# Dense products two chunks at a time in 64-row tiles of TensorE, in a transformer layer on one core

## The chip, the core and the metric
The kernel runs on one core of one Trainium2 chip. TensorE (PE) multiplies, VectorE (DVE), ScalarE (ACT) and GpSimd (POOL) work on its results, and SyncE (SP) issues most transfers. The time is device microseconds of one execution of the program; the kernel before took 677.64 us, the median of three runs (675.79 to 679.14).

## What is computed
For each of 8 rows of 512 tokens x 256 channels, all in float32:

```python
xn = _layernorm(x, axis=-1)
qkv = xn @ qkv_w + qkv_b                       # 16 heads of 16 channels
attn = softmax(einsum('bnhd,bmhd->bhnm', q, k) * scale)
out = einsum('bhnm,bmhd->bnhd', attn, v) @ proj_w + proj_b
gate = xn @ wg.T; up = xn @ wu.T               # 768 hidden, integer weights / 127
ffn = (silu(gate) * up) @ wd.T
x = x + out + ffn
```

## The kernel before
All engines run the same plan. A row has 16 steps: step s handles key tile s % 4 of the head group s // 4, which has four heads in two pairs. A step has two halves, one for each pair of heads. In a half PE computes transposed scores (`scores_t`, L733, into `st_bank`), which ACT turns into `probs` (`exp`, L454), and, six steps ahead (`LEAD`), plain scores (`scores`, L750, into `s_bank`), of which DVE takes the maxima (`maxima`, L575). Each of these is a pair of matmuls in the two 64-row tiles of the array, one for each head, in two banks. `s_bank` and `st_bank` exist once, so the next scores wait for DVE, and the next transposed scores for ACT. Between the halves stands `P @ V` (`probs_v`, L764), in 32-column tiles. The four maxima groups of a row (`max`) are transposed, split and sent by DMA into the rows of `q_stack` that the transposed scores read.

The rest of the layer is cut into chunks: `xn` (transposes of the normalised row), `q`, `k`, `v`, `gate`, `up`, `down`, `proj`, `max`, `o` and `ot` (transposes of the attention's output). A chunk fills one of three banks (`dense`), in turn, by the order of the list `STEADY` (for the first row, in which only chunks and the first scores run, `FIRST`). An entry (step, slot, kind, index, offset) puts the chunk in slot 0 (before the first half), 1 (before the second) or 2 (after it) of a step, for the row at that offset. The same table orders PE, ACT, DVE and POOL: in each slot ACT and DVE first do their part of the half (`exp`; `maxima`), then take the chunks (`take`). A gate chunk is taken by a tanh on ACT (L484) and a product on DVE (L625, `gated`); an up chunk by a product on DVE (L633, `hid`), whose high part ACT copies (L503) and whose low part POOL makes (L413); q and k by ACT (L470) and DVE (L591). DVE's release of a chunk counts in `dense_free`, and a chunk that wants a bank waits for the release of the chunk three before it (L784).

A product is split into exact high and low parts in fp32r, by the list `SPLIT`. As the integer weights are exact in one part, rows 0 to 7 use two terms for gate, up and down, in place of three. `product` (L769) issues a chunk's matmuls one behind the other over all 128 rows of the array. In the first row ACT also squares the low parts of the three integer weights (`square_lows`, L497), by which that is decided, behind `wdown` 2.

## Time and profile before
| | |
|---|---|
| median of 3 runs | 677.64 us |
| profiled execution, its own time | 674.83 us |
| its span | 673.0 us |
| mean granted TensorE clock | 0.987 |
| PE / DVE / ACT / POOL busy | 93 / 74 / 57 / 20% |
| first row's part (before the first exp) | 60.9 us |
| row 0, rows 1 to 6 each, row 7 | 74.3, 77.3 to 78.2, 60.7 us |
| after the last full step | 12 us |

The span runs from the first to the last instruction. PE's busy time is made of modelled ends of pipelined matmuls, which overlap, so the start-to-start distance of matmuls tells more than their length: a row of the timeline with x2 holds two that follow each other, or, for `st_bank` and `s_bank`, two in the two row tiles at once. `PEld` are weight loads.

### The profile page before, as it was taken

The page shows a single profiled execution, that of the slowest core. Times are in us where ns is not written, and L with a number is a line of the kernel's source. Part 1 is how long each engine was busy: PE and PEld are TensorE (multiplying, and loading weights), DVE is VectorE, ACT ScalarE, POOL GpSimd, SP SyncE. Part 2 cuts the span into 40 slices and gives each one's busy share as a digit, 9 for nine tenths or more (in the row PEclk, how much of TensorE's full clock was granted, in tenths as well). Part 3 has the DMA queues.
Part 4 walks back from the last instruction along what each step waited for, and adds up shares of the span by engine and source line. Part 5 has one row for each costly group of instructions (what it writes and reads, how often), then busy time and mean ns, then how long its engine had stood idle before and what let it go on. Part 6 is the DMA issues. An engine that isn't in the chain of part 4 may idle for free.

```text
span 673.0 us, 11305 instructions
## 1 busy us (share of the span) xinstructions
PE 627.3 (93%) x3792; PEld 349.0 (52%) x3792; DVE 498.6 (74%) x676; ACT 383.8 (57%) x499; POOL 133.8 (20%) x134
## 2 busy tenths in 40 slices
PE   6848999999899999999999999999999999999996
PEld 5625545545555555545454555555465455555443
DVE  4758777877778877778778778777778777787732
ACT  2533664756556655656557555566647565566563
POOL 3151113210142004211133002411132101021100
PEclk9868999999999999999999999999999999999999
DMA  8750154112812145111831037211640118120201
GB/s 276 211 106 1 34 164 123 25 38 95 220 49 48 30 150 134 47 48 46 244 72 46 3 127 186 48 48 32 183 127 21 48 63 220 49 48 2 65 2 34
DMA packets 38076, 59.12 MB, mean 88 GB/s; under 512 B 5792, under 2 KB 21152, under 8 KB 38048
## 3 DMA queue, kind: packets, MB, share of 16 engines
q1 hardware_dynamic: 36896, 58.22, 31.4%
q10 hardware_dynamic: 1152, 0.52, 0.3%
q8 instruction: 18, 0.29, 0.2%
q14 instruction: 10, 0.08, 0.0%
HBM read 37.23 MB, written 20.97 MB: 86 GB/s over the span
## 4 chain that ended last, share of the span: by engine, by line
PE 75%; DVE 9%; ACT 5%; issue 5%; DMA 3%; SPq 1%; ACTq 0%; DVEq 0%
PE dense L774 33%; PE o_bank L764 15%; PE st_bank L733 13%; PE s_bank L750 9%; DVE neg_max L575 4%; DMA q_stack<-max_tl 2%; ACT probs L454 2%; PE dense L810 1%; DMA p_bias<-in_L_attn_proj_b 1%; ACT qk_parts L470 1%; SPq L305 1%; PE dense L788 1%; DVE hid L633 1%; PE dense L814 1%; PE dense L805 1%
## 5 line engine op out<-in xcount | busy, mean ns | idle before, releaser
L454 ACT ACTIVATE probs<-st_bank 128x1024 f32<-128x1024 f32 x250 | 256.0, 1024 | 199.6 <-PE st_bank L733 194.5
L575 DVE TENSOR_REDUCE neg_max<-s_bank 128x2 f32<-128x1024 f32 x250 | 305.5, 1222 | 74.7 <-PE s_bank L750 73.8
L764 PE MATMUL o_bank<-probs,v_ones 128*32 128x512 f32 x1024 | 136.4, 605 | 4.3 <-ACT probs L454 2.4
L733 PE MATMUL st_bank<-q_stack,k_stack 50*128 50x512 f32 x500 | 125.0, 496 | 8.8 <-ACT probs L454 4.3
L750 PE MATMUL s_bank<-k_stack,q_stack 48*128 48x512 f32 x500 | 110.0, 436 | 13.8 <-DVE neg_max L575 13.6
L413 POOL TENSOR_TENSOR hid_tl<-hid,hid_th 128x512 fp32r<-128x512 f32 x48 | 61.7, 1285 | 307.6 <-ACT hid_th L503 307.6
L733 PEld LDWEIGHTS st_bank<-q_stack,k_stack 50*128 50x128 f32 x500 | 46.8, 183 | 125.4 <-ACT probs L454 82.3
L750 PEld LDWEIGHTS s_bank<-k_stack,q_stack 48*128 48x128 f32 x500 | 47.5, 186 | 36.6 <-DVE neg_max L575 34.0
L625 DVE SCALAR_TENSOR_TENSOR gated<-gated,dense 128x512 f32<-128x512 f32 x48 | 32.9, 686 | 21.6 <-ACT gated L484 20.9
L764 PEld LDWEIGHTS o_bank<-probs,v_ones 128*32 128x32 f32 x1024 | 20.3, 108 | 50.7 <-issue 46.9
L427 POOL TENSOR_TENSOR resid<-resid,p_bias 128x256 f32<-128x256 f32 x32 | 22.4, 733 | 121.0 <-DMA resid<-in_L_attn_x 121.0
L591 DVE SCALAR_TENSOR_TENSOR qk_parts<-dense,qk_bias,qk_parts 128x512 fp32r<-128x512 f32 x32 | 23.9, 751 | 20.8 <-ACT qk_parts L470 20.8
L484 ACT ACTIVATE gated<-dense 128x512 f32<-128x512 f32 x48 | 28.6, 595 | 13.8 <-PE dense L774 13.8
L503 ACT ACTIVATE hid_th<-hid 128x512 fp32r<-128x512 f32 x48 | 30.0, 626 | 9.1 <-DVE hid L633 9.1
L774 PE MATMUL dense<-xn_th,w_gh 128*128 128x512 f32 x96 | 34.3, 439 | 0.3 <-DVE w_dl L649 0.3
L405 POOL TENSOR_SCALAR xn<-xn,moments,rstd 128x256 f32<-128x256 f32 x28 | 33.8, 1221 | 1.2 <-POOL rstd L399 1.2
L633 DVE SCALAR_TENSOR_TENSOR hid<-dense,gated 128x512 f32<-128x512 f32 x48 | 32.7, 682 | 0.4
L470 ACT ACTIVATE qk_parts<-dense,qk_bias 128x512 fp32r<-128x512 f32 x32 | 21.8, 685 | 19.5 <-PE dense L774 14.1
L774 PE MATMUL dense<-w_dh,hid_th 128*128 128x256 f32 x192 | 31.4, 299 | 0.0
L774 PE MATMUL dense<-xn_th,w_uh 128*128 128x512 f32 x96 | 31.1, 405 | 0.0
L774 PE MATMUL dense<-xn_tl,w_gh 128*128 128x512 f32 x96 | 30.5, 399 | 0.0
L774 PE MATMUL dense<-xn_tl,w_uh 128*128 128x512 f32 x96 | 29.9, 392 | 0.0
(101 smaller groups left out, 708.5 us busy)
## 6 DMA issues: line engine op xcount, KB each, us to landing
q_spread<-qk_parts SPq DMA_DIRECT2D x16, 512.0 KB, 3.0
k_spread<-qk_parts SPq DMA_DIRECT2D x16, 512.0 KB, 3.5
q_stack<-q_spread SPq DMA_DIRECT2D x64, 128.0 KB, 3.1
k_stack<-k_spread SPq DMA_DIRECT2D x64, 128.0 KB, 3.2
q_stack<-q_spread SPq DMA_DIRECT2D x64, 64.0 KB, 3.2
k_stack<-k_spread SPq DMA_DIRECT2D x64, 64.0 KB, 3.2
resid<-in_L_attn_x SPq DMA_DIRECT2D x8, 512.0 KB, 4.9
xn<-in_L_attn_x SPq DMA_DIRECT2D x7, 512.0 KB, 3.5
```

What stands on the lines that cost most here:

```text
L405: nc.gpsimd.tensor_scalar(xn[:, t, :], xn[:, t, :], moments[:, t, 0:1], rstd[:, t:t + 1], ALU.subtract, ALU.mult).then_inc(xn_done, 1)
L413: nc.gpsimd.tensor_tensor(hid_t[1][:, m, :], hid[:, m % 2, :], hid_t[0][:, m, :].bitcast(F32), ALU.subtract).then_inc(hid_low, 1)
L454: nc.scalar.activation(probs[:, s % 2, 2 * half:2 * half + 2, :], transposed_bank(row, s, half)[:, :, :], ACT.Exp, scale=SCALE).then_inc(e ...
L484: nc.scalar.activation(gated[:, i % 2, :], bank[:, :], ACT.Tanh, scale=0.5 * QUANT).then_inc(act_done, 1)
L503: nc.scalar.activation(hid_t[0][:, m, :], hid[:, m % 2, :], ACT.Copy).then_inc(hid_high, 1)
L575: nc.vector.tensor_reduce(neg_max[:, g % 2, :, NT * pair + qt], score_bank(row, half)[:, :, :], AX_X, ALU.max, negate=True).then_inc(max_d ...
L625: nc.vector.scalar_tensor_tensor(gated[:, i % 2, :], gated[:, i % 2, :], 1.0, bank[:, :], ALU.add, ALU.mult).then_inc(dense_free, 1)
L633: nc.vector.scalar_tensor_tensor(hid[:, i % 2, :], bank[:, :], 0.5 * QUANT ** 3, gated[:, i % 2, :], ALU.mult, ALU.mult).then_inc(dense_fr ...
L733: done = nc.tensor.matmul(transposed_bank(row, s, half)[:, r, :], k_stack[rows, pair, P * kt:P * (kt + 1)], q_stack[rows, pair, :], start= ...
L750: done = nc.tensor.matmul(score_bank(row, half)[:, r, :], q_stack[rows, pair, P * qt:P * (qt + 1)], k_stack[rows, pair, :], start=True, st ...
L764: done = nc.tensor.matmul(o_bank[32 * j:32 * (j + 1), :], v_ones[:, kt, HG * g + j, :], probs[:, (s - 1) % 2, j, :], start=kt == 0, stop=k ...
L774: done = nc.tensor.matmul(bank, stationary(a, k), moving(b, k), start=n == 0 and k == 0, stop=n == len(parts) - 1 and k == tiles - 1)
```

## The change
Dense products are no longer made a chunk at a time over the whole array. Two chunks that go together (gate and up of one index, q and k of one index, v 0 and 1, proj 0 and 1, down 0 and 1, 2 and 3) are made at once in the two 64-row tiles: in the first half the upper rows of the contraction go to the bank of the first chunk and the lower rows to that of the second; in the second half the tiles swap banks. So a bank is never written by both tiles at once, and the second half waits for the end of the first (`half_done`). There are as many matmuls again, of 64 rows. Both chunks are done together, with the last matmul (`dense_done` + 2). A table `WORK` of its own now says where PE works: for v, proj and down the two halves stand in different steps, for gate/up and q/k in one block. v's first half stands at the end of the row before. `STEADY` still orders the other engines and the banks. The transposes of `xn`, `o` and `ot` move to slot 1, behind `P @ V`, and `gate` 4 moves from the row before into step 1. In the first row wdown's transposes stand ahead of q 1 and k 1, gate 1 comes at step 10, gate 4 goes, and the squarings stand behind gate 1.

```diff
-    (11, 0, "gate", 0, 1), (11, 2, "down", 3, 0),
-    (12, 0, "up", 0, 1), (12, 2, "gate", 1, 1),
...
+    (9, 1, "o", 1, 0), (10, 1, "max", 3, 0),
+    (10, 2, "down", 2, 0), (11, 0, "down", 3, 0),
+    (11, 2, "gate", 0, 1), (12, 0, "up", 0, 1),
...
+WORK = [
...
+    (7, 2, "down", 0, 0, 0),
+    (8, 2, "down", 0, 1, 0),
+    (9, 1, "o", 1, None, 0), (9, 2, "down", 2, 0, 0),
+    (10, 1, "max", 3, None, 0), (10, 2, "down", 2, 1, 0),
+    (11, 2, "gate", 0, None, 0),
...
+TOGETHER = {
+    ("v", 0): ("v", 1), ("q", 0): ("k", 0), ("q", 1): ("k", 1), ("proj", 0): ("proj", 1),
+    ("down", 0): ("down", 1), ("down", 2): ("down", 3), **{("gate", i): ("up", i) for i in range(KH)},
+}
...
-SQUARES_AFTER = ("wdown", 2)
+SQUARES_AFTER = ("gate", 1)
...
-            def product(bank, stationary, moving, tiles, parts=SPLIT, moving_low=None):
-                for n, (a, b) in enumerate(parts):
-                    if b == 1 and moving_low is not None:
-                        pe.wait_ge(dense_free, moving_low)
-                    for k in range(tiles):
-                        done = nc.tensor.matmul(bank, stationary(a, k), moving(b, k), start=n == 0 and k == 0,
-                                                stop=n == len(parts) - 1 and k == tiles - 1)
+            def product(terms, half, low=None):
+                for (stationary, moving, bank), first, last, moves_low in terms:
+                    if low is not None and moves_low and half == 0:
+                        pe.wait_ge(dense_free, low)
+                        low = None
+                    done = []
+                    for r in range(2):
+                        c = (r + half) % 2
+                        rows = slice(HALF * r, HALF * (r + 1))
+                        done.append(nc.tensor.matmul(bank[c], stationary[c][rows], moving[c][rows],
+                                                     start=first and half == 0, stop=last and half == 1,
+                                                     tile_position=(HALF * r, 0)))
                 return done
-            def chunk_products(row, chunk, exact):
-                _, _, kind, i, offset = chunk
+            def terms_of(banks, stationary, moving, tiles, parts=SPLIT, column=0, columns=1):
+                return [(([stationary(c, a, k) for c in range(2)], [moving(c, b, k) for c in range(2)], banks),
+                         column == n == k == 0,
+                         column == columns - 1 and n == len(parts) - 1 and k == tiles - 1, b == 1)
+                        for n, (a, b) in enumerate(parts) for k in range(tiles)]
+            def bank_free(row, chunk):
+                if count(Row(row.like, row.like), ALL, chunk) > DENSE_BANKS:
+                    pe.wait_ge(dense_free, count(row, ALL, chunk) - DENSE_BANKS)
+            def two_chunks(row, kind, i, half, exact):
+                (one,), (two,) = named(row, kind, i), named(row, *TOGETHER[kind, i])
+                banks = [bank_of(row, c) for c in (one, two)]
+                if half != 1:
+                    bank_free(row, two)
+                whole = [b[:, :] for b in banks]
+                low = None
+                if kind == "q":
+                    if i == 0:
+                        pe.wait_ge(act_done, count(row, ON_ACT, kind="xn", index=1))
+                        low = count(row, ALL, kind="xn", index=1)
+                    if i == 0 and row.like == -1:
+                        pe.wait_ge(w_low, 2)
+                    terms = terms_of(whole, lambda c, a, k: w_qkv[a][:, k, C * c + P * i:C * c + P * (i + 1)],
+                                     lambda c, b, k: xn_t[b][:, k, :], KC)
+                elif kind == "v":
+                    terms = []
+                    for u in range(2):
+                        terms += terms_of([b[:, C * u:C * (u + 1)] for b in banks],
+                                          lambda c, a, k: xn_t[a][:, k, P * (2 * c + u):P * (2 * c + u + 1)],
+                                          lambda c, b, k: w_qkv[b][:, k, 2 * C:3 * C], KC, column=u, columns=2)
+                elif kind == "gate":
+                    if row.like == -1 and i == 0:
+                        pe.wait_ge(dense_free, count(row, ALL, kind="wup", index=2))
+                    terms = terms_of(whole, lambda c, a, k: (w_g, w_u)[c][a][:, k, P * i:P * (i + 1)],
+                                     lambda c, b, k: xn_t[b][:, k, :], KC, STATIONARY_EXACT if exact else SPLIT)
+                elif kind == "down":
+                    if i == 0 and half == 0:
+                        pe.wait_ge(hid_high, KH * (row.at + 1))
+                        pe.wait_ge(hid_low, KH * (row.at + 1))
+                    terms = terms_of([b[:, 0:C] for b in banks],
+                                     lambda c, a, k: hid_t[a][:, k, P * (i + c):P * (i + c + 1)],
+                                     lambda c, b, k: w_d[b][:, k, :], KH, MOVING_EXACT if exact else SPLIT)
+                else:
+                    if half == 0:
+                        pe.wait_ge(dense_free, count(row, ALL, kind="ot", index=1))
+                    terms = []
+                    for u in range(2):
+                        terms += terms_of([b[:, C * u:C * (u + 1)] for b in banks],
+                                          lambda c, a, k: ot_parts[:, k, a, P * (2 * c + u):P * (2 * c + u + 1)],
+                                          lambda c, b, k: w_p[b][:, k, :], KC, column=u, columns=2)
+                if half != 1:
+                    for done in product(terms, 0, low):
+                        done.then_inc(half_done, 1)
+                if half != 0:
+                    pe.wait_ge(half_done, 2 * count_together(row, kind, i))
+                    product(terms, 1)[1].then_inc(dense_done, 2)
+            def transposes(row, kind, i):
+                (chunk,) = named(row, kind, i)
+                offset = chunk[4]
                 bank = bank_of(row, chunk)
-                n = count(row, ALL, chunk)
...
-                for chunk in chunks_at(row, s, slot):
-                    chunk_products(row, chunk, exact)
+                for step_at, slot_at, kind, i, half, ahead in (FIRST_WORK if row.like == -1 else WORK):
+                    table = of_row(row, ahead)
+                    if (step_at, slot_at) != (s, slot) or table.like > ROWS or not named(table, kind, i):
+                        continue
+                    if (kind, i) in TOGETHER:
+                        two_chunks(table, kind, i, half, exact)
+                    else:
+                        transposes(table, kind, i)
```

How PE's instructions move. First, row 0, the blocks of gate 1 with up 1 (step 12), before. The names are the tiles: `w_gh`, `w_uh` are the weights, `xn_th`, `xn_tl` the high and low part of the transposed row.

```order
L750 MATMUL s_bank<-k_stack,q_stack 128x512 x2
L774 MATMUL dense2<-xn_th,w_gh 128x512 x2
L774 MATMUL dense2<-xn_tl,w_gh 128x512 x2
L774 MATMUL dense0<-xn_th,w_uh 128x512 x2
L774 MATMUL dense0<-xn_tl,w_uh 128x512 x2
L733 MATMUL st_bank<-q_stack,k_stack 128x512 x2
```

The same place on PE in the changed kernel, from the last pair of the first half on:

```order
L826 MATMUL dense2<-xn_tl,w_gh 128x512
L826 MATMUL dense0<-xn_tl,w_uh 128x512
L826 MATMUL dense0<-xn_th,w_uh 128x512
L826 MATMUL dense2<-xn_th,w_gh 128x512
L826 MATMUL dense0<-xn_th,w_uh 128x512
L826 MATMUL dense2<-xn_th,w_gh 128x512
L826 MATMUL dense0<-xn_tl,w_uh 128x512
L826 MATMUL dense2<-xn_tl,w_gh 128x512
L826 MATMUL dense0<-xn_tl,w_uh 128x512
L826 MATMUL dense2<-xn_tl,w_gh 128x512
L778 MATMUL st_bank<-q_stack,k_stack 128x512 x2
```

Gate's bank (`dense2`) was complete four matmuls ahead of the end; now it is written until the last matmul, like up's. Second, PE in step 13 of row 0, where `o` 2 is transposed, before:

```order
L764 MATMUL o_bank<-probs,v_ones 32x512 x4
L733 MATMUL st_bank<-q_stack,k_stack 128x512 x2
L750 MATMUL s_bank<-k_stack,q_stack 128x512 x2
L810 MATMUL dense1<-ident,o_raw 128x128 x4
L774 MATMUL dense2<-xn_th,w_gh 128x512 x2
```

and in the changed kernel:

```order
L809 MATMUL o_bank<-probs,v_ones 32x512 x4
L908 MATMUL dense1<-ident,o_raw 128x128 x4
L778 MATMUL st_bank<-q_stack,k_stack 128x512 x2
L795 MATMUL s_bank<-k_stack,q_stack 128x512 x2
L826 MATMUL dense2<-xn_th,w_gh 128x512
```

The transposes, which use the whole array, moved from the dense block to the place between `P @ V` and the 64-row pairs.

## Rows read from the trace of the kernel before
**Rows 1.** The page, part 1: busy us (share of the span) and instructions
```profile
PE 627.3 (93%) x3792; PEld 349.0 (52%) x3792; DVE 498.6 (74%) x676; ACT 383.8 (57%) x499; POOL 133.8 (20%) x134
```

**Rows 2.** Stretches: length, busy us (x) of PE, PEld, DVE, ACT, POOL, clock, DMA
```profile
290.06:305.25 15.19, 13.91 (x91) 7.58 (x91) 11.57 (x17) 8.63 (x12) 2.25 (x2) 1.00 0.15 39
305.25:325.43 20.18, 20.16 (x124) 11.53 (x123) 15.54 (x18) 12.29 (x17) 1.41 (x2) 1.00 0.26 94
325.43:344.25 18.82, 18.00 (x117) 9.95 (x116) 15.23 (x26) 9.95 (x12) 5.27 (x8) 1.00 0.72 180
344.25:367.40 23.15, 23.15 (x136) 12.12 (x135) 18.42 (x22) 15.45 (x21) 7.70 (x7) 1.00 0.17 43
...
60.92:135.20 74.28, 72.09 (x422) 38.84 (x420) 57.25 (x77) 45.14 (x58) 16.33 (x17) 0.98 0.29 80
...
600.40:661.10 60.70, 55.76 (x365) 27.98 (x363) 35.33 (x47) 37.34 (x45) 5.90 (x7) 1.00 0.11 27
```

**Rows 3.** Timeline, steps 1 and 2: start, us, engine, line, operation
```profile
298.08 0.40 PE L774 MATMUL dense<-w_qkvl,xn_th 128*128 128x256 f32 x2
...
298.32 0.40 PE L774 MATMUL dense<-w_qkvh,xn_th 128*128 128x256 f32 x2
...
300.06 0.50 PE L733 MATMUL st_bank<-q_stack,k_stack 50*128 50x512 f32 x2
300.17 0.19 PEld L750 LDWEIGHTS s_bank<-k_stack,q_stack 48*128 48x128 f32 x2
300.40 0.40 PE L750 MATMUL s_bank<-k_stack,q_stack 48*128 48x512 f32 x2
...
300.73 1.07 PE L764 MATMUL o_bank<-probs,v_ones 128*32 128x512 f32 x8
...
301.73 0.28 PE L805 MATMUL dense<-ident,neg_max 128*16 128x128 f32 x1
...
301.93 0.50 PE L733 MATMUL st_bank<-q_stack,k_stack 50*128 50x512 f32 x2
```

**Rows 4.** Timeline, steps 12 and 13 of a full row
```profile
275.80 0.60 ACT L484 ACTIVATE gated<-dense 128x512 f32<-128x512 f32 x1
275.99 0.61 PE L774 MATMUL dense<-xn_tl,w_uh 128*128 128x512 f32 x2
...
276.43 0.69 DVE L625 SCALAR_TENSOR_TENSOR gated<-gated,dense 128x512 f32<-128x512 f32 x1 [0.60 <-ACT gated L484]
...
276.54 0.50 PE L733 MATMUL st_bank<-q_stack,k_stack 50*128 50x512 f32 x2
...
277.32 1.23 DVE L575 TENSOR_REDUCE neg_max<-s_bank 128x2 f32<-128x1024 f32 x1 [0.20 <-PE s_bank L750]
...
278.46 0.68 DVE L633 SCALAR_TENSOR_TENSOR hid<-dense,gated 128x512 f32<-128x512 f32 x1
...
278.60 0.51 PE L750 MATMUL s_bank<-k_stack,q_stack 48*128 48x512 f32 x2
```

**Rows 5.** Timeline, step 0 of a full row
```profile
290.93 0.68 DVE L625 SCALAR_TENSOR_TENSOR gated<-gated,dense 128x512 f32<-128x512 f32 x1
...
291.52 1.22 DVE L575 TENSOR_REDUCE neg_max<-s_bank 128x2 f32<-128x1024 f32 x1
...
292.80 0.50 PE L750 MATMUL s_bank<-k_stack,q_stack 48*128 48x512 f32 x2 [0.55 <-DVE neg_max L575]
```

**Rows 6.** The page, part 5: DVE's half of q and k
```profile
L591 DVE SCALAR_TENSOR_TENSOR qk_parts<-dense,qk_bias,qk_parts 128x512 fp32r<-128x512 f32 x32 | 23.9, 751 | 20.8 <-ACT qk_parts L470 20.8
```

**Rows 7.** Timeline, the end of the program
```profile
669.77 0.69 DVE L645 TENSOR_TENSOR resid<-dense,resid 128x512 f32<-128x512 f32 x1 [0.74 <-PE dense L774]
```

**Rows 8.** Timeline, first row
```profile
38.40 0.69 DVE L625 SCALAR_TENSOR_TENSOR gated<-gated,dense 128x512 f32<-128x512 f32 x1 [5.58 <-ACT gated L484]
...
41.99 0.80 PE L750 MATMUL s_bank<-k_stack,q_stack 48*128 48x512 f32 x2 [7.57 <-DVE neg_max L575]
...
60.38 0.51 PE L733 MATMUL st_bank<-q_stack,k_stack 50*128 50x512 f32 x2 [0.96 <-DVE neg_max L575]
```

More of the change, by code:

```diff
@@ L138, in count, with count_together @@
     return total + sum(PER_ROW[kind] for kind in kinds) * (row.at - like)
+def count_together(row, kind, index):
+    mine = [c[2:4] for c in chunks_of(row.like) if c[2:4] in TOGETHER]
+    total = sum(c[2:4] in TOGETHER for r in range(-1, row.like) for c in chunks_of(r))
+    return total + mine.index((kind, index)) + 1 + len(TOGETHER) * (row.at - row.like)
 OFFSET = {c[2:4]: c[4] for c in STEADY}
@@ L268, in chunks_at, with named @@
             return [c for c in chunks_of(row.like) if c[:2] == (step, slot)]
+        def named(row, kind, i):
+            return [c for c in chunks_of(row.like) if c[2:4] == (kind, i)]
         def pair_ahead(row, step, half):
@@ L512, in hidden_highs, with maxima_taken @@
                                 hidden_high(r, chunk)
+            def maxima_taken(row, s, slot):
+                if slot == 0:
+                    s, slot = s - 1, SLOTS
+                return [c for c in chunks_at(row, s, slot - MAX_DELAY) if c[2] == "max"]
             def load_max(row, chunk):
@@ L539, in step @@
                                 square_lows()
-                        for chunk in chunks_at(row, s, slot - MAX_DELAY):
-                            if chunk[2] == "max":
-                                load_max(row, chunk)
+                        for chunk in maxima_taken(row, s, slot):
+                            load_max(row, chunk)
                         if slot == 1 and s % NT == 0 and 0 < STEPS * row.like + s <= STEPS * ROWS:
@@ L780, in chunk_products @@
+            def transposes(row, kind, i):
+                (chunk,) = named(row, kind, i)
+                offset = chunk[4]
                 bank = bank_of(row, chunk)
-                n = count(row, ALL, chunk)
-                if count(Row(row.like, row.like), ALL, chunk) > DENSE_BANKS:
-                    pe.wait_ge(dense_free, n - DENSE_BANKS)
+                bank_free(row, chunk)
                 if kind == "xn":
@@ L788, in chunk_products @@
                         done = nc.tensor.transpose(bank[:, P * t:P * (t + 1)], xn[:, t, P * i:P * (i + 1)], ident[:, :])
-                elif kind in ("q", "k"):
-                    if kind == "q" and i == 0:
-                        pe.wait_ge(act_done, count(row, ON_ACT, kind="xn", index=1))
-                    if i == 0 and row.like == -1:
-                        pe.wait_ge(w_low, 1 if kind == "q" else 2)
-                    base = (0 if kind == "q" else C) + P * i
-                    low = count(row, ALL, kind="xn", index=1) if kind == "q" and i == 0 else None
-                    done = product(bank[:, :], lambda a, k: w_qkv[a][:, k, base:base + P],
-                                   lambda b, k: xn_t[b][:, k, :], KC, moving_low=low)
-                elif kind == "v":
-                    for u in range(2):
-                        t = 2 * i + u
-                        done = product(bank[:, C * u:C * (u + 1)], lambda a, k: xn_t[a][:, k, P * t:P * (t + 1)],
-                                       lambda b, k: w_qkv[b][:, k, 2 * C:3 * C], KC)
                 elif kind == "max":
@@ L815, in chunk_products @@
                                                    ident[:, :])
-                elif kind in ("gate", "up"):
-                    w = w_g if kind == "gate" else w_u
-                    if kind == "gate" and count(Row(row.like, row.like), ("gate",), chunk) == 1:
-                        pe.wait_ge(dense_free, count(Row(-1, -1), ALL, kind="wup", index=2))
-                    done = product(bank[:, :], lambda a, k: w[a][:, k, P * i:P * (i + 1)],
-                                   lambda b, k: xn_t[b][:, k, :], KC, STATIONARY_EXACT if exact else SPLIT)
-                elif kind == "down":
-                    if i == 0:
-                        pe.wait_ge(hid_high, KH * (row.at + 1))
-                        pe.wait_ge(hid_low, KH * (row.at + 1))
-                    done = product(bank[:, 0:C], lambda a, k: hid_t[a][:, k, P * i:P * (i + 1)],
-                                   lambda b, k: w_d[b][:, k, :], KH, MOVING_EXACT if exact else SPLIT)
-                elif kind == "proj":
-                    if i == 0:
-                        pe.wait_ge(dense_free, count(row, ALL, kind="ot", index=1))
-                    for u in range(2):
-                        t = 2 * i + u
-                        done = product(bank[:, C * u:C * (u + 1)], lambda a, k: ot_parts[:, k, a, P * t:P * (t + 1)],
-                                       lambda b, k: w_p[b][:, k, :], KC)
                 elif kind == "wdown":
```

43 lines of the change are left out of this document (27 added, 16 removed), and 17 rows, old and new, of tables (FIRST, STEADY).

## The prediction
> **What bounds the kernel now.** I read the busy times first: PE is busy 93% of the span [rows 1]. Then a table by stage of one of the six full rows (77.3 us each): steps 0 to 2 take 15.19 us, 3 to 6 20.18, 7 to 10 18.82, 11 to 15 23.15; row 0 takes 74.3 us and row 7 60.7 [rows 2]. PE is nearly gap-free in the last three stages, DVE is second at 60.8 of 77.3 us. Then the timeline, start to start, for what PE's time is made of. Full-array products of 512 columns follow each other every 0.23 us, of 256 columns every 0.12 [rows 3, 4]. The pairs of 64-row tiles behave otherwise when they follow another shape: `st_bank` starts 0.32 after the last dense matmul, its weights are then loaded in the open (the load for `s_bank` begins 0.11 later), and `s_bank` starts 0.34 after it, though only 0.23 after its own load began; `P @ V` starts 0.33 after that; from its start to what follows is 1.00 [rows 3, 4]. So a change of tile shape costs about 0.2 us (0.1 to drain, 0.1 of open weight load), and each step ends with two of them, 64-row to full and back.
>
> **The change, part by part.**
> Dense products in 64-row tiles. Both changes at the end of each step go: 2 x 0.2 = 0.39 us, 16 times a row: -6.3 us. The pairs are taken at 0.23 (512 columns) and 0.12 (256), as full-array products are. Bounds: 0.23 below, as nothing in the rows streams 512 columns faster, and 0.34 above, if the load is never hidden [rows 3]; I take 0.23, since the load of `s_bank` began 0.11 after `st_bank` in the same row tiles and cost nothing more. On this the Trainium skill (TensorE: Matmul & The Clock Gate, "The mechanism") is stricter: a weight load overlaps matmuls in flight only when the row group differs. The rows speak against that rule here; by it every pair would cost 0.11 more, which is a rival below.
>
> Halves. A half waits until the other half of the same two banks is done. Where other work stands between (v, proj, down) this is free. For six gate/up and two q/k blocks it stands inside the block: the last matmul takes 0.40 from start to end, 0.05 for the hand-over, 0.11 for an open load, in place of 0.23: +0.32, 8 times: +2.6 us. Bounds: 0 to 0.4 each.
>
> Small transposes beside `P @ V`. There they sit between a 32-column and a 64-row shape: six more visits at 0.2 us: +1.2 us; the four of `max` were there already [rows 3]. PE's own work so falls by 2.5 us a row: by these distances it is 72.8 now (the other 4.5 are waits) and 70.3 then.
>
> What comes late instead. A gate and its up product now finish together. Before, gate was done 0.93 us ahead of the end of the block, and its tanh (0.60) ran beside up [rows 4]. Now, counted from the end D of the block: tanh 0.05 to 0.65, DVE `gated` from 0.68, DVE maximum from 1.28 to 2.51 (a DVE instruction behind another starts 0.1 before the end of the first), and the second `s_bank` of the step, which waits for that maximum, at 2.56. PE alone would be there at -0.165 + 0.23 + 0.33 + 1.00 + 0.34 = 1.73. So PE waits 0.83 us in each of the six steps after a gate block. Step 0 of before shows it, where the gate product is already the last of a block: `gated` runs first on DVE, the maximum starts at 291.52 behind it, and the next `s_bank` waits 0.55 for it [rows 5]. A gate block is then 0.34 + 3 x 0.23 + 0.45 + 0.11 + 3 x 0.23 + 0.40 = 2.68 from `s_bank` to D, so a step takes 5.24, where it took 4.5 to 4.9.
>
> Banks. Two chunks need two of three banks at once, so a block waits for the release of the chunk three before its second. In steps 13, 14 and 15 that is `hid` of the last block, at 2.41 + 0.68 = 3.09 on DVE [rows 4]: the block starts at 3.14 with an open load, D at 5.59. In step 2 it is `max` (5.78), in step 3 the low half of the first `xn` (5.46), in step 6 k of the last block (DVE 0.75 each [rows 6]: 6.74), in step 9 `o`, since down's half now stands ahead of it (4.81). Transfers: those of the `max` rows are issued by ACT behind q 1 as now, and are needed at step 8; I count nothing for them, as the block before and step 7 cover them, and if they land late the cost is a wait at the first `st_bank` of step 8.
>
> Sum. Worked through in this way the steps are: 0 to 2: 3.80, 5.35, 5.78 = 14.93 (before 15.19); 3 to 6: 5.46, 3.73, 5.81, 6.74 = 21.74 (20.18); 7 to 10: 4.65, 3.70, 4.81, 3.77 = 16.93 (18.82); 11 to 15: 4.47, 5.24, 5.59, 5.59, 4.85 = 25.74 (23.15). Together 79.3 against 77.3: **+2.0 us a row**. Steps with no release in the way gain 0.4 to 1, those behind gate and q/k lose as much. Six rows: +12. Row 0 has no `o`, `ot`, `proj` of a row before, so it had less to gain and has the same gate blocks: +3. Row 7 has no gate 0 to 3 and no q/k: -2. The end: both proj chunks finish together, so the first 0.69 us addition no longer runs beside the second product [rows 7], and one open half wait: +1.
>
> First row. Before, three squarings on ACT stand ahead of gate 1's tanh, DVE waits 5.58 us for it, and PE then 7.57 for the first maximum [rows 8]. They move behind gate 1, and that wait goes. But wdown now stands ahead of q 1 and k 1, gate 0 ends some 6 us later by my count, and each later gate ends with its up, behind which DVE waits for tanh, and v's first half is added. I come out at 60.4 us for the first score of row 0, where it is now [rows 8]: 0, between -6 (the wait goes and nothing replaces it) and +3.
>
> Total +14 us on the profiled execution, whose own time is 674.8 us (span 673.0, 1.8 us around it). The median of the runs is 677.6, 2.8 above it. 674.8 + 14 is 689; half the offset added: **690 us**.
>
> **Rivals.**
> A, forecast: the freed time is spent in waits for releases and in half waits. 678 to 708, as a row comes out at +0.5 to +4.
> B, PE's saved changes are kept for the most part: the tanh chain is overlapped better than I think (ACT is busy only 57% of the time [rows 1]), and q/k and proj steps come out at PE's time. PE's own sum with the present waits is 2.5 us a row less, 17 in seven rows: 657 with nothing from the first row, 651 with its 6; without any wait it would be 626. For it: 16 changes a row are certain to go, and PE is the busy engine. Against it: step 0 of before [rows 5], where this order of events already stalls.
> C, both sides cancel: within 0.5% (3.4 us, about what a measurement of this kernel can tell from no change). 675 to 681.
> D, weight loads of 64-row tiles aren't hidden in a long stream: 0.11 more for each pair. A row has 72 pairs of 512 and 96 of 256 columns, some 120 of them on the path: +13 us a row, some 780. Against it: rows 3. For it: no stretch of this trace has more than two such pairs in a row, nor four instructions in 0.12 us for long.
> E, the 0.2 us isn't a matter of shape but of any hand-over between these products: nothing goes, +6.3 us a row more than in A, some 735. Against it: full-array products of different tiles follow at 0.12 and 0.23 without a gap.
>
> **Chances.** A 0.53, D and E together 0.08: slower 0.61. C 0.12 is no change, B 0.27 faster. The range: 0.1 of the chance lies under 652 (the better part of B), 0.1 above 714 (D, E and a row at +5). A's own range is 678 to 708.
>
> **What would show it.** Right: rows of 78 to 81 us; the two shape changes gone (dense to `st_bank` 0.23, `st_bank` to `s_bank` 0.23 at the start of a step); steps 12 to 15 of 5.2 to 5.6 us with PE idle before the second `s_bank`, put down to DVE `neg_max`, some 0.8 us each; a pause of 0.2 to 0.3 us inside gate/up and q/k; DVE waits for `gated` about 0.7 us in each gate step; step 6 the longest. PE busy under 90%. Wrong: rows under 76 us, or no PE wait on `neg_max` in steps 12 to 15; then the chain from tanh to the maximum is not on the path. Pair spacing of 0.34 inside a block would make it D, 0.34 after a dense block E. A first row that ends before 57 us would show that the late gate 0 costs nothing.

## The result, and the profile after

The changed kernel takes 713.99 us (median of four runs, 710.60 to 717.77) against 677.26 for the kernel before: a ratio of 1.054, 95% interval 1.048 to 1.060. It is slower, as forecast, but by 36.7 us where the forecast had 12.7 (690 less 677.3). Its profiled execution has a span of 711.3 us, 38.3 more than before. One run of e12 below, 770.6 us, was in a slower state of the chip and is left out there.

The busy times and the chain of waits of the kernel after, against [rows 1]:

```profile
span 711.3 us, 14030 instructions
## 1 busy us (share of the span) xinstructions
PE 625.4 (88%) x5150; PEld 352.8 (50%) x5150; DVE 492.9 (69%) x676; ACT 385.0 (54%) x499; POOL 133.7 (19%) x134
...
## 4 chain that ended last, share of the span: by engine, by line
PE 57%; DVE 15%; issue 12%; ACT 9%; DMA 4%; ACTq 1%; DVEq 1%; POOL 0%; SPq 0%; POOLq 0%
PE dense L826 35%; PE o_bank L809 8%; DVE neg_max L620 6%; PE st_bank L778 6%; PE s_bank L795 5%; ACT gated L524 4%; DMA q_stack<-max_tl 4%; DVE hid L678 3%; ACT probs L494 2%; ACT qk_parts L510 1%; PE dense L908 1%; DVE qk_parts L636 1%; DVE xn_tl L631 1%; ACTq L566 1%; DVE stats L602 1%
```

PE does the same work in the same busy time and stands idle for 12% of the span instead of 7%; its share of the chain falls from 75 to 57%. The table by stage of one full row of the kernel after, then row 0 and row 7, answers to [rows 2], columns as there (a stage begins with the first `st_bank` product of its step; row 0 and row 7 from their first exponential):

```profile
226.59:241.89 15.30, 14.23 (x117) 7.76 (x115) 11.85 (x17) 8.66 (x12) 2.43 (x2) 1.00 0.15 41
241.89:263.97 22.08, 20.59 (x175) 11.88 (x173) 15.39 (x19) 11.95 (x16) 1.30 (x1) 1.00 0.28 96
263.97:282.62 18.65, 15.98 (x169) 9.68 (x165) 14.23 (x23) 10.22 (x12) 4.05 (x7) 1.00 0.66 170
282.62:308.46 25.84, 23.82 (x183) 12.26 (x180) 18.48 (x23) 15.55 (x21) 8.80 (x8) 1.00 0.15 39
65.49:146.60 81.11, 73.08 (x570) 39.42 (x568) 57.22 (x77) 45.41 (x59) 16.27 (x17) 0.96 0.27 74
636.60:697.78 61.18, 52.27 (x457) 26.89 (x455) 35.14 (x47) 37.70 (x45) 6.12 (x7) 1.00 0.10 27
```

This row takes 81.87 us, in stages of 15.30, 22.08, 18.65 and 25.84, where the forecast had 14.93, 21.74, 16.93 and 25.74. In the sum of the span the 38.3 us lie so: up to the first exponential 65.5 us instead of 60.9 (+4.6), row 0 81.1 instead of 74.3 (+6.8), rows 1 to 6 490.0 instead of 465.2 (+24.8), row 7 61.2 instead of 60.7 (+0.5), the end 13.5 instead of 12.0 (+1.5).

A step behind a gate block in the timeline of the kernel after (start, duration, engine and line, what it writes and reads; in brackets the idle time before it and what ended it):

```profile
286.88 0.39 PE L826 MATMUL dense<-xn_tl,w_gh 64*128 64x512 f32 x1
...
287.11 0.39 PE L778 MATMUL st_bank<-q_stack,k_stack 50*128 50x512 f32 x2
...
287.32 0.60 ACT L524 ACTIVATE gated<-dense 128x512 f32<-128x512 f32 x1 [1.59 <-PE dense L826]
...
287.94 0.69 DVE L670 SCALAR_TENSOR_TENSOR gated<-gated,dense 128x512 f32<-128x512 f32 x1 [1.61 <-ACT gated L524]
288.55 1.22 DVE L620 TENSOR_REDUCE neg_max<-s_bank 128x2 f32<-128x1024 f32 x1
...
289.82 0.50 PE L795 MATMUL s_bank<-k_stack,q_stack 48*128 48x512 f32 x2 [0.44 <-DVE neg_max L620]
...
290.17 0.39 PE L826 MATMUL dense<-xn_th,w_gh 64*128 64x512 f32 x1
...
290.40 0.39 PE L826 MATMUL dense<-xn_th,w_gh 64*128 64x512 f32 x1
290.40 0.18 PEld L826 LDWEIGHTS dense<-xn_tl,w_gh 64*128 64x128 f32 x1
...
290.63 0.39 PE L826 MATMUL dense<-xn_tl,w_gh 64*128 64x512 f32 x1
...
290.86 0.39 PE L826 MATMUL dense<-xn_tl,w_gh 64*128 64x512 f32 x1
...
291.34 0.18 PEld L826 LDWEIGHTS dense<-xn_th,w_uh 64*128 64x128 f32 x1 [0.52 <-PE dense L826]
...
292.37 0.39 PE L778 MATMUL st_bank<-q_stack,k_stack 50*128 50x512 f32 x2
```

This is the forecast's chain, event by event. The block ends at 287.27 (286.88 + 0.39); tanh at +0.05, `gated` at +0.67, the maximum at +1.28, the second `s_bank` at +2.55 (forecast 2.56). The pairs follow at 0.23; between the halves PE's queue stands until 291.34, 0.48 after the last pair; from dense to `st_bank` it is 0.23 where [rows 3] had 0.32. The step takes 5.26 us (forecast 5.24). The waits of the kernel after, in total, times and longest:

```profile
DVE gated L670 <- ACT gated L524: 78.1, 47, 3.5
...
DVE qk_parts L636 <- ACT qk_parts L510: 46.4, 23, 4.8
...
PEld dense L826 <- PE dense L826: 34.3, 65, 0.8
...
PEld st_bank L778 <- DMA q_stack<-max_tl: 6.6, 5, 2.1
```

DVE waits 78.1 us for tanh; in the kernel before it was 20.9; for the q and k takes 46.4, before 20.8. The last line is the wait for the max rows, which the forecast priced at nothing. It is not new. The same view of the kernel before has:

```profile
PEld st_bank L733 <- DMA q_stack<-max_tl: 5.2, 4, 2.0
```

What such a wait costs in either kernel is the matter of e1 and e7. In the row above it looks so:

```profile
264.18 0.69 ACT L510 ACTIVATE qk_parts<-dense,qk_bias 128x512 fp32r<-128x512 f32 x1 [3.54 <-PE dense L826]
264.18 0.51 ACTq L566 DMA_DIRECT2D q_stack<-max_th  x1
...
264.72 0.52 ACTq L566 DMA_DIRECT2D q_stack<-max_tl  x1
...
265.42 1.02 ACT L494 ACTIVATE probs<-st_bank 128x1024 f32<-128x1024 f32 x1 [0.56 <-issue]
...
270.05 0.19 PEld L778 LDWEIGHTS st_bank<-q_stack,k_stack 50*128 50x128 f32 x2 [1.42 <-DMA q_stack<-max_tl]
```

ACT issues the two transfers of the max rows behind its take of q 1. That product now ends with k 1, so they go out at 264.18 and 264.72, among the stack transfers; the exponential of step 7 stands 0.56 us behind their issue, and `st_bank` of step 8 waits 1.42 for the second.

### The profile page after: what moved, and what is told of

It is laid out like the page before. It is cut to its first block, busy times and chain, and to the rows that moved or that the text cites. A ratio compares the mean times of both kernels' runs of the same rounds, so it can differ in the third digit from the quotient of the medians.

```text
span 711.3 us, 14030 instructions
## 1 busy us (share of the span) xinstructions
PE 625.4 (88%) x5150; PEld 352.8 (50%) x5150; DVE 492.9 (69%) x676; ACT 385.0 (54%) x499; POOL 133.7 (19%) x134
## 4 chain that ended last, share of the span: by engine, by line
PE 57%; DVE 15%; issue 12%; ACT 9%; DMA 4%; ACTq 1%; DVEq 1%; POOL 0%; SPq 0%; POOLq 0%
PE dense L826 35%; PE o_bank L809 8%; DVE neg_max L620 6%; PE st_bank L778 6%; PE s_bank L795 5%; ACT gated L524 4%; DMA q_stack<-max_tl 4%; DVE hid L678 3%; ACT probs L494 2%; ACT qk_parts L510 1%; PE dense L908 1%; DVE qk_parts L636 1%; DVE xn_tl L631 1%; ACTq L566 1%; DVE stats L602 1%
## 5 line engine op out<-in xcount | busy, mean ns | idle before, releaser
L809 PE MATMUL o_bank<-probs,v_ones 128*32 128x512 f32 x1024 | 138.0, 611 | 8.0 <-ACT probs L494 4.7
L778 PE MATMUL st_bank<-q_stack,k_stack 50*128 50x512 f32 x500 | 113.8, 451 | 21.4 <-ACT probs L494 14.3
L670 DVE SCALAR_TENSOR_TENSOR gated<-gated,dense 128x512 f32<-128x512 f32 x48 | 33.0, 687 | 78.1 <-ACT gated L524 78.1
L826 PE MATMUL dense<-xn_th,w_gh 64*128 64x512 f32 x192 | 68.6, 437 | 6.0 <-DVE max_tl L653 2.0
L826 PE MATMUL dense<-xn_th,w_uh 64*128 64x512 f32 x192 | 68.6, 437 | 4.3
L826 PE MATMUL dense<-xn_tl,w_gh 64*128 64x512 f32 x192 | 60.5, 395 | 0.0
L826 PE MATMUL dense<-xn_tl,w_uh 64*128 64x512 f32 x192 | 60.5, 395 | 0.0
L636 DVE SCALAR_TENSOR_TENSOR qk_parts<-dense,qk_bias,qk_parts 128x512 fp32r<-128x512 f32 x32 | 23.8, 749 | 46.4 <-ACT qk_parts L510 46.4
L826 PEld LDWEIGHTS dense<-xn_th,w_uh 64*128 64x128 f32 x192 | 30.8, 189 | 25.7 <-PE dense L826 25.6
L826 PEld LDWEIGHTS dense<-xn_th,w_gh 64*128 64x128 f32 x192 | 30.9, 189 | 15.2 <-DVE hid L678 6.2
L826 PEld LDWEIGHTS dense<-xn_tl,w_gh 64*128 64x128 f32 x192 | 36.0, 187 | 4.4
L826 PEld LDWEIGHTS dense<-xn_tl,w_uh 64*128 64x128 f32 x192 | 35.9, 187 | 4.2
```

Source lines behind the costliest of these rows:

```text
L636: nc.vector.scalar_tensor_tensor(qk_parts[i][:, which, 1 - high, :], bank[:, :], qk_bias[:, KC * which + i:KC * which + i + 1], qk_parts[i ...
L670: nc.vector.scalar_tensor_tensor(gated[:, i % 2, :], gated[:, i % 2, :], 1.0, bank[:, :], ALU.add, ALU.mult).then_inc(dense_free, 1)
L778: done = nc.tensor.matmul(transposed_bank(row, s, half)[:, r, :], k_stack[rows, pair, P * kt:P * (kt + 1)], q_stack[rows, pair, :], start= ...
L809: done = nc.tensor.matmul(o_bank[32 * j:32 * (j + 1), :], v_ones[:, kt, HG * g + j, :], probs[:, (s - 1) % 2, j, :], start=kt == 0, stop=k ...
L826: done.append(nc.tensor.matmul(bank[c], stationary[c][rows], moving[c][rows], start=first and half == 0, stop=last and half == 1, tile_pos ...
```

## Experiments

All were timed beside the kernel before on the same chip; its medians there were 676.3 to 677.8. The ratio is to these, with its 95% interval. Differences between two variants are of their medians; the intervals are 1 to 4 us to either side, so a difference of 1 or 2 us between two variants says nothing. A step is counted from its first `st_bank` to the next one's, unless said otherwise. In e1 to e4 and e12 one thing is changed in the kernel after.

**e1.** The max transfers issued ahead of ACT's take at the same place.
```
                         hidden_highs(row, SLOTS * s + slot)
+                        for chunk in maxima_taken(row, s, slot):
+                            load_max(row, chunk)
                         for chunk in chunks_at(row, s, slot):
...
-                        for chunk in maxima_taken(row, s, slot):
-                            load_max(row, chunk)
```


> The kernel after with one thing moved on ScalarE: the two transfers of the max rows are issued ahead of the q, gate or xn that ScalarE takes at the same place, not behind it. Theory T1 (the late max rows are what the forecast left out): in the kernel after they are issued only when q 1 and k 1 are done, land some 5 us later among the head transfers, and the first st_bank of step 8 waits 0.8 to 2.1 us in rows 2 to 6; and while ScalarE issues them (2 x 0.5 us) the exponential of steps 3, 7 and 15 starts late. Issued 3 us earlier the waits at step 8 go (7 us in all) and three exponentials a row start 0.5 us sooner (up to 10 us): 714 falls to 697 to 702, and no row is longer than 80.5 us. Rival T2 (the landing is set by the traffic of the head transfers, the time of issue is indifferent; the late exponentials are covered by DVE): 708 to 714, waits on the max transfer stay.

705.2 us, ratio 1.039 (1.035 to 1.044): 8.8 us less. In the same row of e1:

```profile
261.74 0.51 ACTq L566 DMA_DIRECT2D q_stack<-max_th  x1
...
262.29 0.62 ACTq L566 DMA_DIRECT2D q_stack<-max_tl  x1
...
265.61 1.02 ACT L494 ACTIVATE probs<-st_bank 128x1024 f32<-128x1024 f32 x1
...
269.37 0.22 PEld L778 LDWEIGHTS st_bank<-q_stack,k_stack 50*128 50x128 f32 x2
```

Counted from the start of the row (226.59 in the kernel after, 227.62 in e1) the transfers go out 3.5 us sooner. No `st_bank` waits for them any more, and rows 1 to 6 take 480.4 us, 9.6 less than after: 6.4 in step 7, 2.0 in step 8 and 1.2 in step 0. T1 holds for the waits and hardly for its second half. The exponentials start sooner, but counted from exponential to exponential steps 2 and 3 take 11.07 us instead of 11.08 together, and 14 and 15 10.29 instead of 10.28; only step 0, behind the late exponential of step 15, is 0.2 us shorter. So T1's sum of 12 to 17 was too high.

**e2.** The kernel after with the first row in the old order (q 1, k 1 and gate 0 ahead of wdown, gate 1 at step 8, squares behind wdown).
```
-    (4, 0, "wdown", 0, 1), ... (5, 0, "q", 1, 1), (6, 0, "k", 1, 1), (7, 0, "gate", 0, 1), (7, 2, "up", 0, 1),
-    (10, 2, "gate", 1, 1), (11, 0, "up", 1, 1),
+    (4, 0, "q", 1, 1), (5, 0, "k", 1, 1), (6, 0, "gate", 0, 1), (6, 2, "up", 0, 1),
+    (7, 0, "wdown", 0, 1), ... (8, 0, "gate", 1, 1), (8, 2, "up", 1, 1),
...
-SQUARES_AFTER = ("gate", 1)
+SQUARES_AFTER = ("wdown", 2)
```


> The kernel after with the first row in the order of the kernel before as far as pairs allow: wdown behind up 0, q 1 and k 1 ahead of gate 0, gate 1 at step 8, squares behind wdown 2. Theory T3 (the new order of the first row costs more than the squares' wait gives back, because each gate now runs between maxima and the later start of gate 0 pushes all behind it): the first exponential comes at 61 to 62 us instead of 65.5, and the whole is 3 to 5 us shorter, 709 to 711. Rival T4 (the order is indifferent, the products in pairs that end together are what costs): the first exponential at 65 to 67 us, 713 to 716.

722.3 us, 1.064 (1.059 to 1.069): 8 us slower, the first exponential at 72.9 us. Both theories fall. The new order isn't what costs in the first row: in the kernel after it saves 7.4 us up to the first exponential.

**e3.** Gate and up as full-array products, one after the other.
```
-    ... **{("gate", i): ("up", i) for i in range(KH)},
...
+                    elif kind in ('gate', 'up'):
+                        single(table, kind, i, exact)
```


> The kernel after with gate and up undone alone: each is a full-array product again, gate first, and its tanh may start while up runs; v, q, k, proj and down stay in 64-row pairs. Theory T5 (what costs is the chain from the end of both chunks over tanh and gated to the maximum): steps 12 to 15 fall from 5.3, 5.6, 5.6, 4.9 to 4.5 to 4.9 each, steps 2 and 3 by 0.3 to 0.5 each, DVE's wait for gated from 78 us to some 20; 3 us a row, 22 to 27 us in all: 687 to 692. Rival T6 (the shape changes that come back cost as much as the chain, 0.39 a step in six steps): 708 to 716.

682.6 us, 1.007 (1.004 to 1.010): 31.4 us less, more than T5 said. From the end of step 13 on, in e3:

```profile
362.34 0.59 ACT L524 ACTIVATE gated<-dense 128x512 f32<-128x512 f32 x1
362.51 0.61 PE L913 MATMUL dense<-xn_tl,w_uh 128*128 128x512 f32 x2
...
362.97 0.69 DVE L670 SCALAR_TENSOR_TENSOR gated<-gated,dense 128x512 f32<-128x512 f32 x1 [0.31 <-ACT gated L524]
...
363.06 0.50 PE L778 MATMUL st_bank<-q_stack,k_stack 50*128 50x512 f32 x2
...
363.84 1.23 DVE L620 TENSOR_REDUCE neg_max<-s_bank 128x2 f32<-128x1024 f32 x1 [0.18 <-PE s_bank L795]
```

Tanh runs beside the last up products again, `gated` is at work when `st_bank` starts, and the maximum follows 0.78 us behind `st_bank`; in the kernel after it was 1.44 (288.55 less 287.11). DVE's wait for tanh falls to 22.1 us.

**e4.** Gate and up in full-array products, turn about, both released at the end.
```
...
+                if kind == "gate":
+                    for (stationary, moving, bank), first, last, _ in terms:
+                        for c in range(2):
+                            done = nc.tensor.matmul(bank[c], stationary[c], moving[c], start=first, stop=last)
+                    done.then_inc(dense_done, 2)
+                    return
```


> The kernel after with gate and up as full-array products that still end together: first term of gate, first term of up, and so on, both chunks released at the end. No half wait inside the block, and a change of shape at either end. With e3 it parts the order of the ends from the shape of the tiles. Theory T5: the chain behind the end of the block is as in the kernel after, the block itself 0.3 us shorter (no half wait) and 0.1 to 0.2 longer at its start; 700 to 714, far from e3. Rival T7 (the half wait and the 64-row tiles are what makes gate and up slow): close to e3, 686 to 695.

705.1 us, 1.039 (1.035 to 1.044). T5 holds: of the 31.4 us, 22.5 lie between e4 and e3, which differ in when gate is ready and released, and 8.9 in the half wait and the tiles. Steps 12 to 14 are 5.09, 5.25, 5.25 here, 5.26, 5.62, 5.62 after: 0.37 a block in steps 13 and 14, where the bank of the last `hid` decides, as the forecast's 0.32 had it.

**e5.** e3, and q and k the same way. **e6** is e5 with e1's edit. **e11** has q and k single, gate and up in pairs.
```
-    (5, 2, "q", 0, None, 0),
+    (5, 2, "q", 0, None, 0), (5, 2, "k", 0, None, 0),
...
-    ("q", 0): ("k", 0), ("q", 1): ("k", 1),
...
```


> As e3 (gate and up full-array products one after the other), and q and k too: only v, proj and down are left in 64-row pairs, whose halves stand in different steps. Theory T5 (a product pays for ending together with its partner whenever engines stand ready for the first of the two): e3 still has steps 5 and 6 of 6.4 and 7.4 us where the kernel before has 5.5 and 4.9 with the same work; with q released ahead of k ScalarE and VectorE take it while k runs, and the two steps lose 2 us a row: 664 to 671, under the kernel before. Rival T6 (steps 5 and 6 are long because two products, a transpose and the releases lie there, not because they end together): 678 to 684.

> e5 and e1 in one: gate, up, q, k as full-array products, the transfers of the max rows issued ahead of ScalarE's take. If the two gains are independent, 8 to 9 us under e5: 656 to 663. If the early end of q already lets the transfers go out in time, 2 to 4 us under e5: 661 to 668.

> The kernel after with q and k alone as full-array products, gate and up in pairs. With after, e3 and e5 it completes a table of two by two. If the costs of the two are independent: 714.0 less the 26.6 between e3 and e5, 685 to 690. If part of the 26.6 was there only because gate and up had left (the wait for the max transfer and the late exponentials are covered by other waits in the kernel after): 692 to 700.

e5: 656.0 us, 0.968 (0.965 to 0.970), faster than the kernel before and more than T5 said. e11: 690.6, 1.020 (1.017 to 1.023), between its two forecasts. So gate and up in pairs cost 31.4 us beside paired q and k and 34.6 beside single ones; q and k cost 26.6 and 23.4. The two are nearly independent. The 26.6 hold the late transfers of the max rows as well: from e3 to e5 step 7 falls from 5.85 to 3.86 us. e6: 657.4, 0.972 (0.969 to 0.975), no gain over e5: where q is released ahead of k, the transfers are late no longer. A full row of e5 by stage:

```profile
284.87:299.48 14.61, 13.77 (x101) 7.50 (x97) 11.41 (x17) 9.13 (x14) 1.80 (x2) 1.00 0.20 46
299.48:319.71 20.23, 19.92 (x150) 11.80 (x149) 16.69 (x21) 12.77 (x17) 2.06 (x2) 1.00 0.29 105
319.71:336.17 16.46, 15.91 (x167) 9.77 (x167) 13.83 (x23) 9.54 (x11) 4.06 (x7) 1.00 0.80 192
336.17:358.94 22.77, 22.77 (x151) 12.18 (x147) 18.84 (x24) 15.09 (x21) 8.71 (x7) 1.00 0.16 41
```

74.07 us against 77.34 in [rows 2] and 81.87 after. Steps 7 to 10, with down in pairs whose halves lie in different steps, take 16.46 instead of 18.82; PE is busy 22.77 of 22.77 us in the last five steps.

**e7.** The kernel before with e1's edit. **e8.** The kernel before with the first row's order of the kernel after: e2's diff the other way round. Gate 3, gate 4 and the first max transpose keep their places of the kernel before.


> The kernel before with e1's one edit. Its profile has waits of st_bank on the max transfer too (6.6 us in 5 places) and late exponentials behind the issues. If e1's gain has nothing to do with the pairs: 5 to 9 us faster, 669 to 673. If it is there only because q and k end together in the kernel after: 676 to 679.

> The kernel before with the first row's order of the kernel after (wdown ahead of q 1, squares behind gate 1, gate 1 at step 10), products as before. e2 took this order out of the kernel after and lost 8 us, so in the kernel after it is worth 8. Theory T8: it is worth as much with full-array products: the first exponential at 53 to 56 us instead of 60.9, 669 to 673 in all. Rival T9: in the kernel before the old order was in tune with its products; within 2 us of 677.8.

e7: 679.6 us, 1.003 (1.001 to 1.005). Nothing is gained, though the weight loads of `st_bank` wait only 1.8 us for the max rows instead of 5.2. In row 3 the transfers go out 1.1 us sooner, counted from the row's start, and q 1 is taken 0.5 us later. In the kernel before, a wait at the end of step 7 is also made good in step 8: the two take 4.34 and 5.26 us in row 2, where nothing waits, and 5.43 and 4.55 in row 4. In the kernel after they take 4.67 and 3.95 in row 1 and, with the wait, 6.08 and 3.82 in row 2: nothing comes back. What makes it good in the kernel before was not looked into.

e8: 670.4, 0.989 (0.987 to 0.991), T8 holds: the first exponential comes at 55.5 us instead of 60.9.

**e9.** e5 with v, proj and down as full-array products at the places of the halves.
```
-                if half != 1:
-                    bank_free(row, two)
+                bank_free(row, (one, two)[half])
...
+                for (stationary, moving, bank), first, last, _ in terms:
+                    done = nc.tensor.matmul(bank[half], stationary[half], moving[half], start=first, stop=last)
+                done.then_inc(dense_done, 1)
+                return
```


> e5 with v, proj and down as full-array products too, each chunk at the place where e5 has a half of the two (the same work at each place; down 2 is then taken one place earlier). Nothing is left of the 64-row tiles in the dense products; order and places are e5's. Theory T10 (what e5 gains over the kernel before are the changes of tile shape): 8 steps a row get 0.39 us back, 3 us a row, 18 to 25 us in all: 674 to 681. Rival T11 (the gain comes from the order: transposes beside P @ V, other places): 654 to 660.

661.7 us, 0.978 (0.975 to 0.982): 5.7 above e5, between the two theories and far nearer to T11. Steps 4, 7, 8, 10 and 15 are 0.25 to 0.5 longer than in e5 (4.25, 4.1, 4.1, 4.1, 4.55 against 3.73, 3.85, 3.85, 3.76, 4.27); the forecast had 0.39 for the two changes of shape. But steps 1, 3 and 9 are 0.3 to 0.45 shorter (4.94, 4.97, 4.54 against 5.38, 5.27, 4.97). A pair needs two of the three banks at once: in e5 weight loads of the halves wait 7.2 us for `o_norm` and 4.5 for `xn_tl`, in e9 for neither. Over half of the saving goes back in that way. The rest of e5's gain over the kernel before (21.2 us in all) comes without any pair: 6.7 from the order of the first row (e8), and 8.7 between e8 and e9, which differ in the places of the chunks.

**e10.** e5 with `o` 3, `ot` 1, `o` 0 and `o` 2 behind the scores, ahead of the full-array product.
```
-    (1, 1, "o", 3, None, 0), ... (2, 1, "ot", 1, None, 0), ... (5, 1, "o", 0, None, 0), ... (13, 1, "o", 2, None, 0),
+    (1, 2, "o", 3, None, 0), ... (2, 2, "ot", 1, None, 0), ... (5, 2, "o", 0, None, 0), ... (13, 2, "o", 2, None, 0),
```


> e5 with the small transposes o 3, ot 1, o 0 and o 2 moved from beside P @ V to where full-array products follow them (ahead of gate 4, gate 5, q 0 and gate 2). Theory T12 (a visit of full-array work between P @ V and the next st_bank costs 0.2 us, the forecast's term of 1.2 a row for six): four visits go, 0.8 us a row: 648 to 652. Rival T13 (o is then released later, and the products that take its bank, and VectorE's maxima, wait): 656 to 662.

651.2 us, 0.962 (0.959 to 0.966), the lowest of all. The time lies in T12's range, but by luck: the full rows stay at 74.0. Step 1 is 0.2 shorter and step 5 0.2 longer; `o` is released later there (T13). What the edit gives is in row 7 (60.3 to 58.4 us), where no full-array product stands behind the transposes. The other part isn't the edit's. The first exponential comes 1.9 us sooner (59.5 for 61.4), with the same instructions ahead of it and a granted clock of 0.72 for 0.67 from 40 to 60 us. And step 5 of row 0 falls from 8.15 to 6.60, where e13, in the same order, has 7.94: in e5 `P @ V` takes 1.94 us there instead of 1.06, with the granted clock at its lower level from 84.0 to 87.5 us. So the 4.8 us between e5 and e10 are in part scatter of the clock. The forecast's 1.2 us a row for six visits beside `P @ V` is not to be had by moving four of them.

**e12.** The kernel after with the first max transpose at step 14, slot 1. **e13.** e10 with that and with e1's edit.
```
-    (13, 2, "max", 0, 1),
+    (14, 1, "max", 0, 1),
```


> The kernel after with one number changed in the first row: the first max transpose at step 14, slot 1 (where the kernel before has it), not at step 13, slot 2. There TensorE stands 3.9 us for the eighth maximum with step 14's scores behind it, and the next products run at half clock (pairs 0.42 us apart). Theory T14 (this stand is a good part of the 10 us that separate the first exponential of after, 65.5 us, from e8's 55.5): the first exponential 2 to 4 us sooner, 709 to 712. Rival T15 (VectorE's and ScalarE's chain over the late gates sets the pace, TensorE's stand is only its shadow): the first exponential within 1 us of 65.5, 712.5 to 715.

> e10 with the first max transpose at step 14, slot 1, as in e12, and its transfers issued ahead of ScalarE's take, as in e1. e10 has its first exponential at 59.5 us where e8, with the same order otherwise, has 55.5. If e12's theory T14 holds also with full-array gates: 2 to 3 us less than e10's 651.2, 648 to 650. If not: 650 to 652.

e12: 710.5 us (median of three), 1.052 (1.047 to 1.057). The time lies in T14's range, the first exponential, at 64.5 us one sooner, at T15's edge, and the interval doesn't part e12 from the kernel after. So the two theories stay undecided; the stand is worth 1 us at most in these two profiles. It isn't gone either: PE stands 2.17 and 1.22 us there instead of 3.90. e13: 652.9, 0.965 (0.961 to 0.968), no gain on e10.

The timeline of the first row after shows the chain that T15 means:

```profile
45.88 0.62 PE L826 MATMUL dense<-xn_th,w_gh 64*128 64x512 f32 x1
...
46.31 0.62 PE L826 MATMUL dense<-xn_th,w_gh 64*128 64x512 f32 x1
...
50.51 0.60 ACT L524 ACTIVATE gated<-dense 128x512 f32<-128x512 f32 x1 [4.11 <-PE dense L826]
...
54.84 0.27 PE L903 MATMUL dense<-ident,neg_max 128*16 128x128 f32 x1 [3.90 <-DVE neg_max L620]
...
55.87 0.63 PE L826 MATMUL dense<-xn_th,w_gh 64*128 64x512 f32 x1
...
56.30 0.63 PE L826 MATMUL dense<-xn_th,w_gh 64*128 64x512 f32 x1
...
60.62 0.60 ACT L524 ACTIVATE gated<-dense 128x512 f32<-128x512 f32 x1 [5.20 <-PE dense L826]
```

The first six pairs of each of these two blocks follow at 0.42 us, not 0.23: the granted clock is 0.50 (1.2 GHz) from 45.6 to 48.9 and from 55.8 to 59.1. Of the last six nearly all follow at 0.23. Ahead of the second block PE stood for 3.90 us, ahead of the first for 0.89, 1.23 and 1.23, and in e12 this block starts at 0.42 too. So a gate block takes 4.6 to 4.8 us (45.88 to 50.51, 55.87 to 60.62), tanh and `gated` come behind it, and only then the next maximum. In e8 gate 3 and up 3 stand in different steps:

```profile
45.93 0.74 PE L774 MATMUL dense<-xn_th,w_gh 128*128 128x512 f32 x2
...
48.20 0.58 ACT L484 ACTIVATE gated<-dense 128x512 f32<-128x512 f32 x1
...
49.76 0.74 PE L774 MATMUL dense<-xn_th,w_uh 128*128 128x512 f32 x2
...
55.00 0.50 PE L733 MATMUL st_bank<-q_stack,k_stack 50*128 50x512 f32 x2 [1.00 <-DVE neg_max L575]
```

Tanh of gate 3 runs at 48.20, ahead of up 3 (49.76), and the last maxima are done at 55. The clock doesn't tell the two apart: from 40 to 60 us it is 0.83 on average in the kernel after and 0.84 in e8.

## Why the forecast was right in sign and wrong in size

The forecast is 24 us short: 12.8 in rows 1 to 6, 4.6 in the first row, 3.8 in row 0, 2.5 in row 7, 0.5 at the end.

- **Shape changes, pair spacing.** Right. 0.23 from dense to `st_bank`, 0.23 and 0.12 between pairs. The sentence on weight loads of the Trainium skill (TensorE: Matmul & The Clock Gate, "The mechanism"), that they overlap matmuls in flight only when the row group differs, doesn't hold here as it stands (the section also lets a load into the background weight buffer go ahead): the load at 290.40 (0.18 us) runs beside the matmul of the same row tiles, and the pairs of 290.40 and 290.63 are 0.23 apart. Rivals D and E are out.
- **Half wait.** 0.32 said. Seen: 0.48 from the last pair to the next half, where the load is open, and 0.34 to its second pair, for 0.23 twice: 0.36. e4 gets back 0.37 a block.
- **Chain over tanh.** Right to 0.02 us in the step, and the largest single cost: 22.5 us (e4 to e3). The 36.7 are what is left of costs and gains together, gate and up 31.4, q and k 26.6 with the late transfers, less the 21.2 by which e5 is under the kernel before. Rival B needed the chain off the path and fell.
- **Banks.** Steps 2, 3, 6, 13 to 15: 5.78, 5.46, 6.74, 5.59, 5.59, 4.85 said; 5.89, 5.51, 6.76, 5.62, 5.62, 4.85 seen. Steps 1, 2, 5 and 9 were 0.1 to 0.3 too low. A full row of e1, where the max transfers are in time, takes 80.2 us, 0.8 above the forecast's row.
- **Transfers of the max rows, the first failed step.** "I count nothing for them." They cost 1.6 us a row (e1). The cover named, the block before and step 7, was none: that block is what delays their issue, as q 1 now ends with k 1. They were not in time in the kernel before either (5.2 us of waits), but there the wait cost little (e7); in the kernel after nothing makes it good. The forecast named the wait at the first `st_bank` of step 8 and gave it no price and no upper bound.
- **Six rows.** +12 said, +24.8 seen: 9.6 are the transfers, some 5 the small terms (0.8 six times), and some 10 are left of what was counted.
- **First row, the second failed step.** 0 said, +4.6 seen. The forecast let a gain of 6 be eaten by the later gate 0, the gates that end with their ups and v's first half. e8 shows that the late gate 0 costs almost nothing: the order as a whole gives 5.4 with full-array products. The rest then costs 10.0 (55.5 to 65.5), not 6. At a like granted clock from 40 to 60 us, 4.5 to 7 of it go with products that end together: 66.4 in e4 and 61.9 in e3 (clock 0.68 and 0.66), 65.5 in the kernel after and 58.3 in e6 (0.83 both). Another 2.6 are there without any pair: 58.1 in e9, 55.5 in e8 (0.84 both). These two differ in the places of gate 3 and the first max transpose, and e9 has v 0 where e8 has gate 4; which of these it is stays open. The lower clock doesn't explain the 10, as e8 has as much of it.
- **Row 0.** +3 said, +6.8 seen. By `st_bank` starts, steps 3 to 6 of row 0 take 17.96 us before, not the 20.18 of a full row, since no `proj` of a row before stands there; q and k in pairs make steps 5 and 6 as long as elsewhere (6.41, 6.76), 21.34 in all: +3.4 where a full row has +1.9. Steps 0 to 2 take 16.48 instead of 14.30, most of it in step 2: 3.66 us before, with no `o` of a row before, 5.63 after. The clock has little part in it (0.80 from 60 to 70 us, 0.83 in the kernel before). The forecast reasoned from what row 0 lacks, not from its own steps.
- **Row 7 and the end.** -2 and +1 said, +0.5 and +1.5 seen. Row 7 still has the blocks of gate 4 and 5.

The five parts (first row, row 0, six rows, row 7, the end) come to 38.2 of the 38.3 us.

## What to carry to other kernels

Two products that share the array should end at different times if an engine waits for the first: ask for each pair who takes the first result, and what stands behind that taker. When a product ends later, move every instruction behind its taker in that queue, the issue of transfers too, and then ask for the landing. Pairs paid here only for v, proj and down, whose halves lie in different steps, and there over half of the gain went into holding two of three banks. And ask of a wait that is there already what makes it good now, and whether the change leaves that in place.

## What was not expected of the hardware

A pair of row tiles takes 0.42 us at the lower clock (granted 0.50, from 55.8 to 59.1 us) instead of 0.23. The first half of a block of 24 matmuls ran so behind a stand of 3.90 us, and also behind shorter ones (0.89 to 1.23 us each): 1.1 us a block. A transfer of 16 rows of 128 numbers took 5.3 us from issue to the end of the wait (264.72 to 270.05) among transfers whose median landing is 3.3 to 3.4 us.
